# Added products of the identity on the tensor engine, in the first norm and the node updates of a graph network

## What is computed

```
h = maximum(layernorm(x), 0);  x = x + L0(h)      # messages: relu(h[src], h[dst] @ W_msg + b), mean by dst;
                                                  # relu([h, mean] @ W_upd + b)
h = maximum(layernorm(x), 0);  x = x + L1(h)      # degree-normalised sum by dst, plus h; @ W.T + b
h = maximum(layernorm(x), 0);  x = x + L2(h)      # attention over edges, @ Wo, norm, MLP with gelu, norm
h = maximum(layernorm(x), 0);  x = x + L3(h)      # expm(-t L) @ h by 4 x 20 Taylor steps
```

## Time and profile before

| | us |
|---|---|
| median of 3 executions | 4954.18 (4951.66 to 4958.89) |
| profiled execution, its own time | 4959.33 |
| its span, first to last instruction | 4957.5 |
| first norm | about 195 (from 498 to 693) |
| node update, layer 0 | about 316 (from 1302 to 1618) |
| node update, layer 1 | about 250 |
| node update, layer 2 | about 775 |

### The profile page before, as it was taken

How to read it: one execution, slowest core, us unless ns; L and a number is a source line. 1 busy time by engine, 2 the same in 40 slices (tenths; PEclk the granted TensorE clock), 3 DMA queues, 4 the chain that set the end, 5 groups by cost and what they waited for, 6 DMA issues and landing times. The chain is left out here.

```text
span 4957.5 us, 53329 instructions
## 1 busy us (share of the span) xinstructions
PE 3171.5 (64%) x11864; PEld 1972.5 (40%) x11864; DVE 2806.8 (57%) x6339; ACT 969.0 (20%) x1858; POOL 2764.1 (56%) x2438
## 2 busy tenths in 40 slices
PE   3664745555799599674777567777636665555424
PEld 1221534444577588452222145555422222222113
DVE  5997762222355544465777547877755555444323
ACT  0132420000122110221222123333311221111100
POOL 0375027777211573335777577777327776787641
PEclk8776565555555555555555555555558887777665
DMA  4332641111355210552222343343212111233215
GB/s 170 125 75 59 242 168 24 24 24 24 87 156 157 46 26 11 179 210 54 41 42 42 63 46 78 81 102 78 67 51 37 37 36 33 30 31 28 24 14 106
DMA packets 336995, 363.14 MB, mean 73 GB/s; under 512 B 236961, under 2 KB 268843, under 8 KB 336864
## 3 DMA queue, kind: packets, MB, share of 16 engines
q1 hardware_dynamic: 222752, 262.46, 16.4%
q0 software_dynamic: 94096, 80.75, 13.5%
q10 hardware_dynamic: 20016, 18.41, 1.1%
HBM read 188.08 MB, written 188.36 MB: 76 GB/s over the span
## 5 line engine op out<-in xcount | busy, mean ns | idle before, releaser
L814 PE MATMUL e_ps<-e_msg,e_hot 128*128 x2408 | 571.2, 424 | 220.9 <-issue 215.3
L814 PEld LDWEIGHTS e_ps<-e_msg,e_hot 128*128 128x128 f32 x2408 | 530.1, 329 | 299.6 <-issue 299.6
L1704 POOL DMA_INDIRECT u_a<-attended,dst_end x392 | 478.3, 1220 | 146.7 <-issue 116.0
L2335 PE MATMUL d_pl<-d_hot,d_fields 128*65 128x512 f32 x712 | 486.2, 848 | 0.0
L787 DVE TENSOR_TENSOR sums<-e_ps,sums 128x455 f32 (+1 forms) x172 | 108.1, 628 | 554.2 <-PE e_ps L814 554.2
L730 POOL DMA_INDIRECT e_msg<-from_src,e_src x200 | 192.1, 960 | 293.6 <-DMA e_first<-lot_first 234.6
L1990 POOL DMA_INDIRECT list<-s_rec,s_place x200 | 200.8, 1004 | 270.3 <-DVE s_place L1906 216.7
L2279 POOL DMA_INDIRECT flows<-d_out,d_end x160 | 264.2, 1651 | 106.8 <-issue 104.2
L2266 POOL DMA_INDIRECT d_near<-term,d_rec x196 | 190.9, 974 | 156.4 <-DMA d_rec<-list 97.0
L909 POOL DMA_INDIRECT a_ends<-h,a_src x200 | 216.8, 1084 | 103.4 <-issue 57.3
L1396 ACT ACTIVATE u_zt<-u_pt 128x256 f32<-128x256 f32 (+1 forms) x392 | 163.0, 432 | 555.8 <-PE u_pt L1296 555.6
(11 more groups left out here) (366 smaller groups left out, 7585.2 us busy)
## 6 DMA issues: line engine op xcount, KB each, us to landing
u_z<-h SPq DMA_DIRECT2D x28, 896.0 KB, 6.2
x<-sums SPq DMA_DIRECT2D x28, 896.0 KB, 8.4
u_x<-x SPq DMA_DIRECT2D x28, 896.0 KB, 7.8
terms<-s_zeros SPq DMA_DIRECT2D x16, 812.5 KB
s_key_row<-src_key SPq DMA_DIRECT2D x50, 256.0 KB, 3.0
h1d<-u_h SPq DMA_DIRECT2D x14, 910.0 KB, 9.4
u_z<-h1d SPq DMA_DIRECT2D x14, 910.0 KB, 4.6
term<-u_h SPq DMA_DIRECT2D x14, 910.0 KB, 3.7
```

The costliest lines, as they stand in the source:

```text
L814: last = nc.tensor.matmul(to, hot[s][:, q, :], rows, start=False, stop=q == LOT - 1)
L1704: pool.indirect_dma_start(A[s][:, j, :], None, net.attended[:, :], bass.IndirectOffsetOnAxis(ap=net.dst_end[:, tile:tile + 1], axis=0)).th ...
L2335: last = nc.tensor.matmul(pl[0:WEIGHT + 1, :], fields[:, j, :], hot[:, j, :], start=j == 0, stop=j == J - 1)
```

## The change

A new function adds products of the identity with itself, four copies side by side as the moving operand, which makes 512 columns. Their result goes to a bank that nothing reads: in the first norm and the node updates of layers 0 and 1 a bank of its own (`unread`), in layer 2 the first half of `pf`, which the next `up` product overwrites. They stand

- in the first norm: 8 ahead of each supertile, behind the wait for `normed`, and 2 behind each group,
- in node update 0: 12 ahead of each supertile, behind the wait for `z_ready`, and 2 behind each group,
- in node update 1: 3 behind each group,
- in node update 2: 6 behind each attention group and 4 behind each MLP group.

That is 308, 364, 294 and 980 products in the four stages. No other instruction is changed.

```
+def fill(nc, net, bank, count):
+    for _ in range(count):
+        nc.tensor.matmul(bank[:, :].rearrange("p (r c) -> p r c", c=P), net.identb[:, :],
+                         net.identb[:, :].unsqueeze(1).to_broadcast([P, J, P]), start=True, stop=True)
...
+        unread = ps("unread")
...
                     pe.wait_ge(normed, r + 1)
+                    fill(nc, net, unread, 8)
                     turn(c, 0, start)
...
                         last.then_inc(mm_done, 1)
+                        fill(nc, net, unread, 2)
...
+        if layer < 2:
+            unread = ps("unread")
...
                         last.then_inc(mm_done, 1)
+                        fill(nc, net, unread if layer < 2 else pf[b][:, 0, :], (2, 3, 6)[layer])
...
                         last.then_inc(mm_done, 1)
+                        fill(nc, net, pf[b][:, 0, :], 4)
...
                         pe.wait_ge(z_ready, c[0] + 1)
+                        if layer == 0:
+                            fill(nc, net, unread, 12)
                         products((Z if layer == 0 else A)[c[1]], (c[0], c[1]), start)
```

## The result

| | us |
|---|---|
| before, median of 4 executions | 4954.52 (4951.66 to 4958.89) |
| changed kernel, median of 4 executions | 5003.74 (4992.74 to 5006.31) |
| ratio | 1.0096, 95% interval 1.0081 to 1.0111 |
| profiled execution, span | 5003.5 (before 4957.5) |

The changed kernel is 49 us slower; the prediction was 4990 us, with 59% for slower. The granted clock did rise, in all four stages. Two views show it: the page's PEclk (row of before in the earlier trace rows), and the stages by windows, with the columns of the earlier trace rows.

What follows compares the result with a forecast made beforehand. The prediction took a tensor engine busy 69% to 91% of the four stages, at about half clock, as the bound; +21 +40 -5 -20 = +36 us gave 4995, forecast as 4990 us (8 in 10: 4880 to 5075).

Steps and rivals of the forecast that it cites:

- rival 3: All four stages: the products leave the clock low, 5489 us; chance 0.05.
- rival 1: All four stages: full speed holds through the waits, -78 us, 4876 us; chance 0.20.
- Rival 2: All four stages: the clock drops, but the products bring it back within a group everywhere, -6 us, 4948 us; chance 0.25.
- First norm, +21: First norm: eight products ahead delay each supertile's first evacuation by 1.7 us; period 15.6 us, +21 us in all.
- Node update 0, +40: Node update 0: full speed lost behind the square's wait in nearly every supertile; period 26.0 us, +40 us in all.
- The three kinds of supertile: Node update 0 periods: 21.0 us at full speed throughout, 28.1 with a drop, 26.3 with the drop a group later.
- periods near 23.5: Node update 0: supertiles where the added products bring full speed back after one group, 23.5 us, weighted one third.
- the sum for 28.1: Node update 0 with a drop: groups 3 to 6 low until 21.4 us, the 12 products 2.6 to 5.1, the rest 2.8.
- Node update 1, -5: Node update 1: two groups on the chain each save 0.6 us, less three products of 0.215; -5 us in all.
- would be late next: Node update 1: GpSimd's products and the loads ahead of them would limit next, after the chain through PE; no size given.
- Node update 2, -20: Node update 2: attention groups' six products hidden, MLP groups faster at full speed; -1.5 us a supertile, -20 us in all.
- one drop: Node update 2 MLP: clock lost once, at the wait behind the square, and back a group later; -2.1 us a supertile.

Runs made afterwards that it cites:

- experiment 1: Changed kernel without the products ahead of supertiles in the first norm (8) and node update 0 (12) and behind MLP groups (4): ratio 1.0066.
- experiment 2: Changed kernel, first norm's 8 products moved into a PE wait, 10 and 14 added there in node updates 0 and 1, attention groups' six removed: ratio 0.9957.
- kernel 4: Kernel before plus: first norm 2 per group; node update 0 ten in the wait, 1 per group; node update 2 ten and twenty ahead of `up`: ratio 0.9875.

## Why the prediction was right, and where it was not

- **The clock.** Right that the products bring 2.4 GHz (rival 3 is out: the 14 at 1488.55 last 3.23 us, 0.23 each) and that it does not hold through the waits (rival 1 is out). Rival 2, full speed back within a group everywhere, is out too: behind 1502.03 it is away for 10 us.
- **First norm, +21.** Right in its main term: the eight are pure path (experiment 1 takes them out and gets 8 x 0.215 back), the evacuation came 4.05 us behind the norm's end for 4.2, the period is 15.55 for 15.6. The steady periods are smaller than forecast, 15.2 and 15.5 in turn (for 15.4 with the clock held and 15.8 with it lost); a first one of 17.7 lifts the mean.
- **Node update 0, +40 for +23.** The three kinds of supertile were sized well: 21.0, 26.3 and 28.1 in the prediction, 21.1, 26.7 to 26.9 and 28.4 in the trace (the wait of 2.5 us behind the square, and the clock low after it, too). The step that failed is their weighting: "So I expect a drop in nearly every supertile." The clock was lost in seven of the twelve and held in five, at 21.1, and periods near 23.5, which had a third of the weight, did not occur. The products ahead, priced only as path, also saved what they cost (experiment 1); that they bring the clock back within the twelve was in the sum for 28.1, but not that without them the next supertile would be low.
- **Node update 1, -5 for -0.7.** The step that failed is that the chain through PE was taken as the bound. It is not: the period is 17.7 to 17.9 in every kernel, at clocks from 0.51 to 0.97. The rows of experiment 2 put the loads and POOL's products, named only as what "would be late next", in its place; that is read and not tried.
- **Node update 2, -20 for +8.** Here the working was wrong in two places. The six products behind an attention group were put at nothing, since they "lie in PE's waiting, which hides them", by 3.1 us of DVE's waiting a supertile. That was a total spread over 14 supertiles of which two had nearly all of it. In the steady part DVE does not wait for PE in these groups, and PE has little waiting in most of them to hide a product in: in the first five of a supertile of the kernel before (3094.7 to 3104.5) it is busy for 9.58 of 9.80 us. Experiment 2 takes the six out: 1.4 us a supertile, 18 us in thirteen, most of the error. The second is the MLP: I had one drop, at the wait behind the square, and full speed back a group later. There is another, behind the wait ahead of the first `up`, and in a long period PE works on for 10 us at 1.2 GHz behind it (first window below); in a short one, behind the same wait of 2.41 us, which ends at 3166.47, 2.4 GHz is there again from 3173 on (second window). What this adds was not measured by itself. The four products there pay for themselves and no more (experiment 1).

```profile
3112.00:3122.00 10.00, 10.00 (x39) 5.98 (x36) 4.68 (x5) 3.32 (x6) 7.90 (x7) 0.50 0.90 202
...
3173.00:3179.00 6.00, 5.75 (x36) 3.36 (x34) 5.67 (x6) 1.64 (x3) 5.09 (x4) 1.00 0.94 267
```

- **What was luck.** The total was near because 17 us too many in node update 0 stood against 28 too few in node update 2, and 4 us came from a part that the change does not touch and that I can't attribute. In the first norm a part of the hit is the long first period: the twelve behind it average 15.4.

The advice of the Trainium skill (TensorE: Matmul & The Clock Gate, Why this matters for your kernels) is to leave no PE-idle gaps above some 3 us between bursts of products. The prediction read it as a rule that only such gaps cost the full rate, and the trace does not agree with that: waits of 2.54 to 2.57 us cost it in seven of twelve periods of node update 0. In the first norm the clock is at 0.50 from 558.2 to 561.4, behind a wait of 1.90 us, and at 1.00 from 543 to 546, behind one of 1.91. So a gap's length alone does not tell. What makes the difference was not tried.

## What to carry to other kernels

Products that are added to keep the tensor engine's clock paid best behind the last instruction that PE can issue before a long wait, in a number a little shorter than that wait: ten in the 2.5 us of node update 0 were free. Where PE comes to the wait at 1.2 GHz they take up to twice the time and outlast it, and the runs differ: eight in the wait of the first norm made it 0.3 us a supertile longer than before, and two behind each group did better; ten ahead of the first `up` of node update 2 still gained 1.2. Behind a semaphore that PE has just been waiting for, the eight of the first norm cost their full time. Between groups, products cost what PE has no waiting for: the 42 a supertile in the attention groups, 9.0 us of PE, cost 1.4. Look first for which engine ends last: a stage that waits for loads or for POOL gains nothing from a faster PE, and its granted clock says nothing of its time. A wait's total says whom to charge only once it is seen where in the stage it lies.

## What the runs showed of the hardware that was not expected

- Time and granted clock part ways: node update 2 is 53.45 us at 0.82 and 51.58 at 0.60; node update 1 is the same at 0.51 and 0.97.
- A stretch in which PE is never idle can stay at 1.2 GHz: 10.00 us busy of 10.00 at 0.50, in f32 groups with two of the added products behind each (1504 to 1514 us). The clock rose to 2.4 GHz while the fourteen in a row behind it ran.
- The floor that gathers set is not a constant. I put it at 48.2 us in node update 2; in kernel 4 POOL has no wait and needs 50.6. One gather takes POOL 0.95 us beside a sum of DVE over a whole supertile (3093.01), and 2.38 beside a scaling of it (3095.51). Over ten supertiles the 280 gathers take 1.281 us each in the kernel before and 1.358 in kernel 4, 2.2 us more a supertile; of a supertile's 28, 8.0 and 9.7 take more than 1.2 us.
